# Mixture-of-experts phase: the shared experts moved to the front, their weights loaded and split apart from the routed ones

## The chip, the cores and the metric

One core of a Trainium2 chip runs the whole kernel. The metric is the device time of one execution in microseconds (us); lower is better. "hi" and "lo" below are the two halves into which a float32 tensor is split, so that a product is made by three fp32r matmuls (hi·hi, hi·lo, lo·hi).

## The reference, cut to what matters

The input is `x`, 8 batches of 512 tokens with 256 features. Four layers follow: a mixture of experts, a layer with ternary weights, attention, and a gated feed-forward layer. The change lies in the first.

```
scores = softmax((x @ wt.T + g @ wg.T) / 2)             # 8 routed experts
topk_w, topk_idx = top_k(scores, 2); topk_w /= topk_w.sum(-1)
y_all = (leaky(x @ w_gate[e]) * (x @ w_up[e])) @ w_down[e]
y = sum over the two chosen experts of topk_w * y_all
p = leaky(x @ sw_gate) * (x @ sw_up) @ sw_down          # 2 shared experts of width 128
moe = y + p
```

`leaky(v)` is max(v, 0.01 v). Then `x = x + (quantised moe) @ ternary.T * scale + bias`, and attention and the feed-forward layer follow.

## The kernel before, in words

All ten experts (`NE = 10`: eight routed, `E`, and two shared, `SHARED`) are computed for all tokens, without gathering; a routed expert's activation is multiplied by a per-token weight that is zero where it was not chosen. This is `moe_phase`, a block of its own: the attention phase starts behind a barrier when all engines have ended it. Work is in steps `s = NE*b + k`, batch `b` and expert `k`. Before, k = 0 to 7 are routed and k = 8, 9 are shared. Each engine runs its own list in program order; semaphores join them.

- **TensorE**: `gate_up(b, k)` is 12 matmuls of 512 columns (L33 to L35), into `ps_gate` and `ps_up`, each with two buffers; `down(b, k)` is 12 of 256 columns into `ps_y`, accumulated over all k. `batch` issues `gate_up` two steps ahead: gate_up(k+2), down(k), and then what belongs to other batches (router of b+1 at k = 0, transposes of logits at 1 and of weights at 4, the ternary layer of b-1 at 2, 4, 6). In batch 0 the matmuls `null_projection` (L686) follow down(0,7).
- **ScalarE**: `leak_part` (0.01 v from `ps_gate`, L207), `hidden_hi` (hi half of the hidden activation, L213), and per batch `split_hi` of the next x, `logits_out`, `exps`, `weights_out`, and in batch 0 `projections_hi` (hi half of the attention's query weights, L219).
- **VectorE**: `leaky` (L453, makes `act_g`), `hidden_lo` of the step before (L458), `hidden` (L471, times `ps_up`), and routing (L376 to L418), quantising and the residual (L444).
- **GpSimd**: `weigh` (L300), `act_w = act_g * wide_w` for a routed expert, and `add_bias` (L305), the ternary bias onto `x_nat`, after the eighth `weigh` of a batch. `hidden` of a routed expert waits for its `weigh`; that of a shared one only for `leaky`.
- **SyncE** issues the transfers in order. `load_x`, `load_nat`, then in batch 0 `load_projections` (L834 to L844: query, key-value and output weights and six small tensors of the attention) behind a wait for `raw_free`, then `spread_weights`.

The weights arrive whole: router, gate, up, down (1.25 MB each of the last three). `weight_hi` (L265, ScalarE) and `weight_lo` (L568, VectorE) split each. VectorE does this after the first batch's routing and then unpacks the ternary codes (L583 to L588). `raw_free` comes after that, since the attention's weights take the place of the raw weights in SBUF. TensorE waits for the split gate and up weights before gate_up(0,0), and for the down weights before `batch(0)`.

In batch 0, `null_picks` (VectorE, behind hidden(0,3), L481 and L487) waits for the six small tensors (`att_in`), `null_products` (GpSimd, L314) follows weigh 5 and 7, and `attention_fills` (memsets, L326) follows weigh 2. In batch 6 (`B - 2`), pieces of the attention's first layer norm (`first_norm`, L807 to L827) stand at k = 1, 5, 7 and 9.

Of the kernel before, what the change touches and what calls it, by code (L numbers as in the profile page):

```python
# [11 lines left out]
ALU = mybir.AluOpType  # L12
# [39 lines left out]
def moe_phase(nc, dram, w, ps, sem):  # L52
# [7 lines left out]
    with ExitStack() as ctx:  # L60
        def sb(name, shape, dt=F32):
# [4 lines left out]
        weights = [(router_raw, w.router_hi, w.router_lo, dram.router_t.rearrange("(c p) e -> p c e", p=P)),  # L66
                   (gate_raw, w.gate_hi, w.gate_lo, dram.gate.rearrange("(c p) m -> p c m", p=P)),
                   (up_raw, w.up_hi, w.up_lo, dram.up.rearrange("(c p) m -> p c m", p=P)),
                   (down_raw, w.down_hi, w.down_lo, dram.down.rearrange("(e p) n -> p e n", p=P))]
        ROUTER, GATE, UP, DOWN = range(4)  # L70
# [34 lines left out]
        with nc.Block() as block:  # L105
            @block.sync
            def _(sp):
# [44 lines left out]
                for n, (raw, _, _, src) in enumerate(weights):  # L152
                    sp.dma_start(raw[:], src).then_inc(sem.raw_in[n], 16)
# [16 lines left out]
            def _(act):  # L170
# [63 lines left out]
                def batch(b, par, behind, ahead):  # L234
                    for k in range(NE):
# [3 lines left out]
                        leak_part(s, k % 2)  # L239
# [53 lines left out]
            def _(pool):  # L293
                def weigh(b, k):
                    s = NE * b + k
# [42 lines left out]
                for m in (w.ident, w.ident_bf):  # L338
# [6 lines left out]
                                        pattern=[[-1, E], [1, E]], channel_multiplier=0).then_inc(sem.ident, 1)  # L345
                pool.wait_ge(sem.small_in, 3 * 16)
                for k in range(E):
# [3 lines left out]
                    if k in (5, 7):  # L351
                        null_products(k // 2 - 2)
# [12 lines left out]
            def _(dve):  # L365
# [95 lines left out]
                def hidden(b, k):  # L461
                    s = NE * b + k
                    dve.wait_ge(sem.u_done, s + 1)
                    if k < E:
                        dve.wait_ge(sem.act_w_ready, E * b + k + 1)
# [4 lines left out]
                    src = act_w if k < E else act_g  # L470
# [45 lines left out]
                def batch(b, par, first, behind, ahead):  # L516
                    for k in range(NE):
                        s = NE * b + k
                        leaky(s, k % 2)
                        if not (first and k == 0):  # L520
                            hidden_lo(s - 1, 1 - k % 2)
                        if first and k in (5, 6):
# [12 lines left out]
                        if ahead and k == 0:  # L535
# [5 lines left out]
                        hidden(b, k)  # L541
                        if first and k == 3:
# [22 lines left out]
                def weight_lo(n):  # L565
                    raw, hi, lo, _ = weights[n]
                    dve.wait_ge(sem.hi_ready, n + 1)
                    nc.vector.tensor_tensor(lo[:], raw[:], f32(hi[:]), ALU.subtract).then_inc(sem.lo_ready, 1)  # L568

                split_lo(0, 0)  # L570
                weight_lo(ROUTER)
                softmax_shift(0)
# [4 lines left out]
                weight_lo(GATE)  # L577
                weight_lo(UP)
                weight_lo(DOWN)

                dve.wait_ge(sem.small_in, 3 * 16)
                for c in range(4):
                    nc.vector.tensor_scalar(codes[:, :, c, :], packed[:], 2 * c, 3, ALU.logical_shift_right,  # L583
                                            ALU.bitwise_and)
                dve.drain()
                nc.vector.tensor_scalar(w.tern[:], codes[:].rearrange("p c k n -> p c (k n)"), -1.0, None, ALU.add)
                dve.drain()
                dve.nop(nofuse=True).then_inc(sem.raw_free, 1)  # L588
# [14 lines left out]
            def _(pe):  # L603
# [130 lines left out]
                logits_to_tokens(0)  # L734
# [1729 lines left out]
```

## Time and profile before

| what | value |
|---|---|
| median of 3 runs | 1364.51 us (1364.46 to 1364.55) |
| the profiled execution, its own time | 1364.32 us |
| its span in the profile | 1362.3 us |
| PE busy over the span | 1228.7 us (90%) |
| DVE, ACT, POOL busy | 1035.1, 774.7, 561.9 us |
| moe_phase in the span | 0 to 444 us |

The profile page gives the busy time of each engine. PE is TensorE's matmuls, PEld its weight loads, DVE VectorE, ACT ScalarE, POOL GpSimd, SPq the queue of SyncE. Times in the timeline are microseconds from the span's start; a line has the start, the duration, the engine, the source line, the operation, the tiles (output first), the shape and the count. In brackets stands how long the engine idled before it, and what released it.

### The profile page before, as it was taken

How to read it: one execution, taken by the hardware profiler on the slowest of the kernel's cores; microseconds unless marked ns; L12 is line 12 of the kernel's file. 1: busy time of each engine (PE TensorE's matmuls, PEld its weight loads, DVE VectorE, ACT ScalarE, POOL GpSimd, SP SyncE). 2: the span in 40 equal slices, each digit the busy share in tenths (PEclk: the TensorE clock that was granted, in tenths of full speed). 3: DMA queues.
4: the chain of work that ended last, by engine and by line, in shares of the span. 5: the costliest groups of instructions: out<-in, count | busy, mean ns of one | idle time of the engine just before them, and what ended most of it. 6: DMA issues, size and time to landing. Idle time of an engine off the chain costs nothing. (4 is left out here: it accounts for less than half of the span.)

```text
span 1362.3 us, 26891 instructions
## 1 busy us (share of the span) xinstructions
PE 1228.7 (90%) x8712; PEld 999.2 (73%) x8712; DVE 1035.1 (76%) x2782; ACT 774.7 (57%) x1974; POOL 561.9 (41%) x842
## 2 busy tenths in 40 slices
PE   3999999999887699999999999999999999987976
PEld 2778888888775478788778877887887888764323
DVE  5666666666744777888887897888888887985987
ACT  3333333233232477777677776776777777654666
POOL 1443333323222676435444444454454454530114
PEclk7999999999999699999999999999999999997988
DMA  6332123112200800001001000010010000102206
GB/s 229 118 102 78 52 89 110 71 54 94 89 6 16 290 28 2 1 2 32 1 1 33 1 9 25 2 32 1 1 33 1 1 17 2 65 17 51 62 32 216
DMA packets 49990, 70.38 MB, mean 52 GB/s; under 512 B 4482, under 2 KB 42627, under 8 KB 47812
## 3 DMA queue, kind: packets, MB, share of 16 engines
q1 hardware_dynamic: 49300, 68.55, 15.3%
q8 instruction: 69, 1.13, 0.3%
q14 instruction: 61, 0.50, 0.1%
q10 hardware_dynamic: 560, 0.20, 0.1%
HBM read 56.54 MB, written 12.19 MB: 50 GB/s over the span
## 5 line engine op out<-in xcount | busy, mean ns | idle before, releaser
L1081 POOL TENSOR_SCALAR scores<-scores,att_rinv 128x128 f32<-128x128 f32 (+3 forms) x512 | 266.1, 536 | 175.1 <-DVE att_rinv L1298 175.1
L1142 ACT ACTIVATE scores<-scores,att_top 128x128 f32<-128x128 f32 (+3 forms) x512 | 281.7, 553 | 84.2 <-DVE att_top L1280 83.3
L1280 DVE CUSTOM_DVE_ANT_0 scores<-ps_y,w_bias_b,w_null_s 128x128 f32<-128x128 f32 x448 | 228.4, 547 | 62.5 <-PE ps_y L1475 58.6
L300 POOL TENSOR_TENSOR act_w<-act_g,wide_w 128x512 f32<-128x512 f32 x64 | 105.7, 1652 | 280.0 <-DVE act_g L453 265.4
L1486 PE MATMUL ps_up<-ident,scores 128*128 128x128 f32 x1280 | 191.1, 276 | 9.9 <-DVE keep L1308 5.5
L213 ACT ACTIVATE hid_hi<-hid 128x512 fp32r<-128x512 f32 x80 | 50.6, 632 | 245.9 <-DVE hid L471 245.9
L1486 PEld LDWEIGHTS ps_up<-ident,scores 128*128 128x128 f32 x1280 | 152.7, 141 | 30.5 <-issue 14.4
L1563 PE MATMUL ps_gate<-w_wo,o_t 128*128 128x256 f32 x512 | 133.9, 382 | 0.0
L33 PE MATMUL ps_y<-w_down_hi,hid_hi 128*128 128x256 f32 x320 | 92.6, 289 | 18.1 <-DVE hid_lo L458 18.1
L453 DVE TENSOR_TENSOR act_g<-ps_gate,leak 128x512 f32<-128x512 f32 x80 | 55.3, 691 | 63.2 <-ACT leak L207 60.5
L1142 ACT ACTIVATION_READ_ACCUMULATOR scores<-scores,att_top 128x1 f32 x512 | 96.8, 189 | 0.0
L1150 ACT ACTIVATE keep<-ps_up 128x128 f32<-128x128 f32 (+3 forms) x128 | 55.9, 437 | 62.8 <-PE ps_up L1486 60.2
L1563 PEld LDWEIGHTS ps_gate<-w_wo,o_t 128*128 128x128 f32 x512 | 86.8, 191 | 6.5 <-issue 0.2
L35 PE MATMUL ps_y<-w_down_hi,hid_lo 128*128 128x256 f32 x320 | 90.1, 282 | 0.0
L34 PE MATMUL ps_y<-w_down_lo,hid_hi 128*128 128x256 f32 x320 | 90.0, 281 | 0.0
L1150 ACT ACTIVATE turned_odd<-ps_up 128x128 f32<-128x128 f32 (+3 forms) x128 | 55.9, 437 | 59.4 <-PE ps_up L1486 58.0
L471 DVE TENSOR_TENSOR hid<-ps_up,act_w 128x512 f32<-128x512 f32 x64 | 44.2, 690 | 54.1 <-PE ps_up L35 26.6
L33 PEld LDWEIGHTS ps_y<-w_down_hi,hid_hi 128*128 128x128 f32 x320 | 60.5, 189 | 29.8 <-DVE hid_lo L458 27.5
L1088 POOL TENSOR_SCALAR w_q_hm<-w_q_hl 64x512 fp32r<-64x512 f32 x62 | 37.2, 612 | 103.9 <-ACT w_q_hl L1165 103.9
L1497 PE MATMUL ps_a<-turned_odd,w_val 128*64 128x128 f32 x1280 | 78.6, 279 | 1.3 <-DVE turned_odd L1308 1.3
L1088 POOL TENSOR_SCALAR q_hm<-q_hl 64x512 fp32r<-64x512 f32 x64 | 38.4, 612 | 94.4 <-ACT q_hl L1165 94.4
L1497 PE MATMUL ps_a<-keep,w_val 128*64 128x128 f32 x1280 | 76.9, 275 | 0.0
(335 smaller groups left out, 3226.9 us busy)
## 6 DMA issues: line engine op xcount, KB each, us to landing
wide_w<-token_w_dram SPq DMA_DIRECT2D x16, 1024.0 KB, 4.7
x_raw<-in_x_t_dram SPq DMA_DIRECT2D x8, 512.0 KB, 3.7
x_nat<-in_x_nat_dram SPq DMA_DIRECT2D x8, 512.0 KB, 4.7
x_dram<-x_nat SPq DMA_DIRECT2D x8, 512.0 KB, 2.9
w_x1t<-x_dram SPq DMA_DIRECT2D x8, 512.0 KB, 4.8
x_tile<-x_dram SPq DMA_DIRECT2D x8, 512.0 KB, 4.6
w_bias_b<-in_bias_dram SPq DMA_DIRECT2D x14, 256.0 KB, 4.3
c_dram<-out_raw SPq DMA_DIRECT2D x7, 512.0 KB, 3.2
```

The costliest lines, as they stand in the source:

```text
L33: pe.matmul(out, w_hi, x_hi, start=start, stop=False, skip_group_check=loose)
L34: pe.matmul(out, w_hi, x_lo, start=False, stop=False, skip_group_check=loose)
L35: return pe.matmul(out, w_lo, x_hi, start=False, stop=stop, skip_group_check=loose)
L300: nc.gpsimd.tensor_tensor(act_w[:, k % 2], act_g[:, k % 2], wide_w[:, k], ALU.mult).then_inc(sem.act_w_ready, 1)
L1081: nc.gpsimd.tensor_scalar(s, s, rinv[:, pp, q, hh:hh + 1], 0.0, ALU.mult, ALU.add).then_inc(sem.p_normed, 1)
L1088: nc.gpsimd.tensor_scalar(q_hm[par][0:D, hh], f32(q_hl[par][0:D, hh]), 1.0, 0.0, ALU.mult, ALU.add).then_inc(sem.qm_ready, 1)
L1142: nc.scalar.activation(s, s, ACT.Exp, scale=-1.0, bias=top[:, pp, q, hh:hh + 1], accum_out=lsum[:, pp, q, hh:hh + 1]).then_inc(sem.exp_don ...
L1150: nc.scalar.activation(turned_of(j, 0, 0, cols), psT[:, 0, 0:cols], ACT.Copy).then_inc(sem.pa_ready, 1)
L1280: dve.tensor_tensor_reduce(scores_of(pp, hh, q), psS[:, hh, 0:n], bias_of(w, h)[:, CAUSAL[q]:CAUSAL[q] + n], 1.0, null_s[:, par, q, h:h + ...
L1486: last = pe.transpose(psT[:, hh, k * P:(k + 1) * P], s[:, k * P:(k + 1) * P], w.ident[:])
L1497: last = pe.matmul(psO[hh * D:(hh + 1) * D, cols], val[:, par, k], turned_of(at, hh, k, P), start=(k == 0), stop=(k == q))
L1563: last = pe.matmul(out, o_t[:, p % 2, cols], w.wo[:, p], start=(p == 0 and i == 0), stop=False, skip_group_check=True)
```

## The change

1. The shared experts become k = 0 and 1, the routed ones k = 2 to 9. So `weigh`, and `add_bias` behind the last of them, come two steps later, and `hidden` waits for `weigh` at k ≥ 2.
2. Gate, up and down weights are laid out with the shared experts' columns first, and are loaded and split in two parts each: the shared part (128x512), then the routed part (128x2048). The shared parts are split ahead of the first batch's softmax; TensorE runs gate_up(0,0) before the transposes of the routing weights.
3. The routed gate and up parts' lo halves are made by VectorE after hidden(0,0), followed by `split_lo` of x(1). The routed down part's lo half is made by GpSimd.
4. The ternary codes are unpacked at k = 2 of batch 0, so `raw_free` comes there; it also waits for GpSimd's part. `projections_hi` goes from k = 2, 3 to 3, 4. `null_products` follows weigh 3 and 5, which is the same s as before.

```diff
-        weights = [(router_raw, ...), (gate_raw, ...), (up_raw, ...), (down_raw, ...)]
+        weights = [(router_raw[:], w.router_hi[:], w.router_lo[:], dram.router_t.rearrange("(c p) e -> p c e", p=P))]
+        for first, end in ((0, SHARED), (SHARED, NE)):
+            cols = slice(first * M, end * M)
+            weights += [(gate_raw[:, :, cols], w.gate_hi[:, :, cols], w.gate_lo[:, :, cols], dram_gate[:, :, cols]),
+                        (up_raw[:, :, cols], w.up_hi[:, :, cols], w.up_lo[:, :, cols], dram_up[:, :, cols]),
+                        (down_raw[:, first:end], w.down_hi[:, first:end], w.down_lo[:, first:end],
+                         dram_down[:, first:end])]
+        ROUTER, GATE, UP, DOWN, GATE_ROUTED, UP_ROUTED, DOWN_ROUTED = range(7)
@@ ScalarE, batch
-                        leak_part(s, k % 2)
+                        if behind or k:
+                            leak_part(s, k % 2)
-                        if not behind and k == 2:
+                        if not behind and k == 3:
                             projections_hi(0)
-                        if not behind and k == 3:
+                        if not behind and k == 4:
                             projections_hi(1)
@@ ScalarE, start
+                weight_hi(GATE)
+                weight_hi(UP)
+                weight_hi(DOWN)
                 logits_out(0)
                 exps(0)
-                weight_hi(GATE)
-                weight_hi(UP)
+                weight_hi(GATE_ROUTED)
+                weight_hi(UP_ROUTED)
+                leak_part(0, 0)
+                weight_hi(DOWN_ROUTED)
                 weights_out(0)
-                weight_hi(DOWN)
@@ GpSimd
-                    s = NE * b + k
+                    s = NE * b + SHARED + k
+                pool.wait_ge(sem.hi_ready, DOWN_ROUTED + 1)
+                raw, hi, lo, _ = weights[DOWN_ROUTED]
+                nc.gpsimd.tensor_tensor(lo, raw, f32(hi), ALU.subtract).then_inc(sem.down_lo_ready, 1)
                 for k in range(E):
                     weigh(0, k)
-                    if k in (5, 7):
-                        null_products(k // 2 - 2)
+                    if k in (3, 5):
+                        null_products(k // 2 - 1)
@@ VectorE, hidden
-                    if k < E:
-                        dve.wait_ge(sem.act_w_ready, E * b + k + 1)
+                    if k >= SHARED:
+                        dve.wait_ge(sem.act_w_ready, E * b + k - SHARED + 1)
@@ VectorE, batch
+                        if first and k == 2:
+                            ternary_codes()
-                        if ahead and k == 0:
+                        if ahead and k == 0 and not first:
                             split_lo(b + 1, 1 - par)
                         hidden(b, k)
+                        if first and k == 0:
+                            weight_lo(GATE_ROUTED)
+                            weight_lo(UP_ROUTED)
+                            split_lo(1, 1)
@@ VectorE, start
+                def ternary_codes():
...
+                    dve.wait_ge(sem.down_lo_ready, 1)
+                    dve.nop(nofuse=True).then_inc(sem.raw_free, 1)
                 weight_lo(ROUTER)
+                weight_lo(GATE)
+                weight_lo(UP)
+                weight_lo(DOWN)
                 softmax_shift(0)
                 route_scores(0)
                 route_ranks()
                 route_weights()
-                weight_lo(GATE)
-                weight_lo(UP)
-                weight_lo(DOWN)
@@ TensorE
+                        if not behind and k == SHARED:
+                            pe.wait_ge(sem.down_lo_ready, 1)
                         down(b, k)
@@ TensorE, start
                 logits_to_tokens(0)
+                pe.wait_ge(sem.lo_ready, DOWN + 1)
+                gate_up(0, 0, 0)
                 weights_to_experts(0)
-                pe.wait_ge(sem.lo_ready, UP + 1)
-                gate_up(0, 0, 0)
                 gate_up(0, 1, 0)
-                pe.wait_ge(sem.lo_ready, DOWN + 1)
+                pe.wait_ge(sem.lo_ready, UP_ROUTED + 1)
                 batch(0, 0, False, True)
```

## Rows read from the trace of the kernel before

**Rows 1.** Busy time by stage: PE, PEld, DVE, ACT, POOL, then granted clock, DMA share, GB/s

```profile
0.00:36.00 36.00, 15.01 (x53) 10.05 (x54) 18.61 (x31) 13.33 (x14) 4.57 (x12) 0.81 0.67 236
36.00:90.00 54.00, 48.60 (x260) 37.84 (x258) 34.92 (x55) 15.55 (x28) 23.22 (x16) 0.97 0.31 106
90.00:350.00 260.00, 253.36 (x1478) 213.30 (x1476) 178.69 (x351) 85.25 (x144) 89.51 (x60) 1.00 0.22 76
350.00:444.00 94.00, 75.33 (x426) 61.19 (x426) 52.11 (x102) 26.25 (x44) 23.91 (x15) 0.94 0.11 40
```

**Rows 2.** Timeline of the start, up to down(0,0)

```profile
12.93 0.68 ACT L182 ACTIVATE logit_t<-ps_a,w_cond_half 8x512 f32<-8x512 f32 x1 [4.07 <-PE ps_a L35]
...
16.99 2.32 ACT L265 ACTIVATE w_up_hi<-up_raw 128x2560 fp32r<-128x2560 f32 x1
...
19.59 0.19 DVE L418 TENSOR_TENSOR token_w<-rank,top 128x32 f32<-128x32 f32 x1
...
22.44 2.82 DVE L568 TENSOR_TENSOR w_up_lo<-up_raw,w_up_hi 128x2560 fp32r<-128x2560 f32 x1
...
25.31 0.80 PE L33 MATMUL ps_gate<-x_hi_first,w_gate_hi 128*128 128x512 f32 x1 [4.45 <-DVE w_up_lo L568]
...
35.97 0.28 PE L33 MATMUL ps_y<-w_down_hi,hid_hi 128*128 128x256 f32 x1
```

**Rows 3.** The window of 2 us in down(0,7), columns as in rows 1

```profile
76.00:78.00 2.00, 2.00 (x10) 1.50 (x10) 0.70 (x2) 0.75 (x2) 0.00 (x0) 0.50 0.63 223
```

**Rows 4.** Timeline: VectorE beside GpSimd in batch 0, and down(0,7)

```profile
29.82 1.22 DVE L370 TENSOR_TENSOR x_lo<-x_raw,x_hi 128x1024 fp32r<-128x1024 f32 x1
...
61.98 1.61 POOL L300 TENSOR_TENSOR act_w<-act_g,wide_w 128x512 f32<-128x512 f32 x1 [0.34 <-DVE act_g L453]
...
62.36 2.31 DVE L476 TENSOR_TENSOR w_wq_lo<-keep,w_wq_hi 128x1024 fp32r<-128x1024 f32 x1
...
71.74 2.36 POOL L305 TENSOR_TENSOR x_nat<-x_nat,w_tern_bias 128x1024 f32<-128x1024 f32 x1
...
71.80 2.85 DVE L458 TENSOR_TENSOR hid_lo<-hid,hid_hi 128x512 fp32r<-128x512 f32 x1
...
74.70 0.56 PE L33 MATMUL ps_y<-w_down_hi,hid_hi 128*128 128x256 f32 x1 [2.12 <-DVE hid_lo L458]
```

**Rows 5.** Timeline: the projections' issue, null_picks, projections_hi(1), down(0,3), down(0,4)

```profile
32.00 0.51 SPq L834 DMA_DIRECT2D keep<-in_wq_dram  x1
...
38.81 0.43 SPq L844 DMA_DIRECT2D w_g_out<-in_g_out_dram  x1
...
47.38 0.47 DVE L487 TENSOR_SCALAR w_null_pick<-w_null_pick,w_null_v 64x8 f32<-64x8 f32 x2
...
47.73 1.05 ACT L219 ACTIVATE w_wq_hi<-keep 128x1024 fp32r<-128x1024 f32 x1
...
50.94 0.39 PE L33 MATMUL ps_y<-w_down_hi,hid_hi 128*128 128x256 f32 x1 [0.45 <-DVE hid_lo L458]
...
57.20 0.39 PE L33 MATMUL ps_y<-w_down_hi,hid_hi 128*128 128x256 f32 x1 [0.81 <-DVE hid_lo L458]
```

**Rows 6.** DMA issues of 30 to 50 us: KB, median us from issue to landing

```profile
w_g_out<-in_g_out_dram SPq DMA_DIRECT2D x1, 128.0 KB, 5.5
```

**Rows 7.** Timeline: layer norm pieces on VectorE, batch 6 (k = 7, k = 9), then attention

```profile
361.23 2.26 DVE L821 SCALAR_TENSOR_TENSOR w_work<-w_work 128x4 f32<-128x4 f32 x1
...
370.75 1.55 DVE L827 TENSOR_SCALAR w_x1t<-w_x1t,w_mean_var,w_work 128x256 f32<-128x256 f32 x4
...
704.58 1.12 DVE L827 TENSOR_SCALAR out_raw<-out_raw,w_mean_var,w_work 128x256 f32<-128x256 f32 x2
```

**Rows 8.** Timeline of batch 7: weigh and hidden of k = 7, down(7,9)

```profile
417.68 1.67 POOL L300 TENSOR_TENSOR act_w<-act_g,wide_w 128x512 f32<-128x512 f32 x1 [2.85 <-DVE act_g L453]
...
419.43 0.69 DVE L471 TENSOR_TENSOR hid<-ps_up,act_w 128x512 f32<-128x512 f32 x1 [1.24 <-PE ps_up L35]
...
430.48 0.39 PE L33 MATMUL ps_y<-w_down_hi,hid_hi 128*128 128x256 f32 x1 [0.36 <-DVE hid_lo L458]
```

More of the change, by code:

```diff
@@ L65, in moe_phase @@
         cond_t, router_g, packed, codes = w.cond_t, w.router_g, w.packed, w.codes
[L66 to L70, printed above, removed]
+        dram_gate, dram_up, dram_down = (dram.gate.rearrange("(c p) m -> p c m", p=P),
+                                         dram.up.rearrange("(c p) m -> p c m", p=P),
+                                         dram.down.rearrange("(e p) n -> p e n", p=P))
+        weights = [(router_raw[:], w.router_hi[:], w.router_lo[:], dram.router_t.rearrange("(c p) e -> p c e", p=P))]
[6 more added lines that the diff above has]
+        ROUTER, GATE, UP, DOWN, GATE_ROUTED, UP_ROUTED, DOWN_ROUTED = range(7)
         x_raw = w.x_raw
@@ L152, in _ @@
                 for n, (raw, _, _, src) in enumerate(weights):
-                    sp.dma_start(raw[:], src).then_inc(sem.raw_in[n], 16)
+                    sp.dma_start(raw, src).then_inc(sem.raw_in[n], 16)
                 load_x(1)
@@ L469, in hidden @@
                         dve.wait_ge(sem.hl_ready, s - 1)
-                    src = act_w if k < E else act_g
+                    src = act_w if k >= SHARED else act_g
                     nc.vector.tensor_tensor(hid[:, k % 2], ps.up[:, k % 2], src[:, k % 2], ALU.mult
@@ L567, in weight_lo @@
                     dve.wait_ge(sem.hi_ready, n + 1)
-                    nc.vector.tensor_tensor(lo[:], raw[:], f32(hi[:]), ALU.subtract).then_inc(sem.lo_ready, 1)
+                    nc.vector.tensor_tensor(lo, raw, f32(hi), ALU.subtract).then_inc(sem.lo_ready, 1)
+                def ternary_codes():
+                    dve.wait_ge(sem.small_in, 3 * 16)
+                    for c in range(4):
+                        nc.vector.tensor_scalar(codes[:, :, c, :], packed[:], 2 * c, 3, ALU.logical_shift_right,
+                                                ALU.bitwise_and)
+                    dve.drain()
+                    nc.vector.tensor_scalar(w.tern[:], codes[:].rearrange("p c k n -> p c (k n)"), -1.0, None, ALU.add)
+                    dve.drain()
+                    dve.wait_ge(sem.down_lo_ready, 1)
+                    dve.nop(nofuse=True).then_inc(sem.raw_free, 1)
                 split_lo(0, 0)
                 weight_lo(ROUTER)
+                weight_lo(GATE)
+                weight_lo(UP)
+                weight_lo(DOWN)
                 softmax_shift(0)
@@ L576, in _ @@
                 route_weights()
-                weight_lo(GATE)
-                weight_lo(UP)
-                weight_lo(DOWN)
[L581 to L588, printed above, removed]
                 batch(0, 0, True, False, True)
@@ L2161, in named_semaphores @@
     sem.lo_ready = new("lo_ready")
+    sem.down_lo_ready = new("down_lo_ready")
     sem.cond_logits = new("cond_logits")
@@ L2285, in named_semaphores @@
     sem.out_done = new("out_done")
-    sem.raw_in = [new(f"raw_in{n}") for n in range(4)]
+    sem.raw_in = [new(f"raw_in{n}") for n in range(7)]
     sem.ffn_in = [new(f"ffn_in{n}") for n in range(3)]
@@ L2436 @@
     dram.router_g_t = given("router_g_t", a["L0_cond_wg"].T)
-    dram.gate = given("gate", np.concatenate([e_first(a["L0_cond_w_gate"]), a["L0_cond_sw_gate"]], axis=1))
-    dram.up = given("up", np.concatenate([e_first(a["L0_cond_w_up"]), a["L0_cond_sw_up"]], axis=1))
-    dram.down = given("down", np.concatenate([a["L0_cond_w_down"].reshape(E * M, H), a["L0_cond_sw_down"]], axis=0))
+    dram.gate = given("gate", np.concatenate([a["L0_cond_sw_gate"], e_first(a["L0_cond_w_gate"])], axis=1))
+    dram.up = given("up", np.concatenate([a["L0_cond_sw_up"], e_first(a["L0_cond_w_up"])], axis=1))
+    dram.down = given("down", np.concatenate([a["L0_cond_sw_down"], a["L0_cond_w_down"].reshape(E * M, H)], axis=0))
     dram.packed_t = given("packed_t", a["L0_ffn_packed_weight"].reshape(H // 4, H).T)
```

2 lines of the change are left out of this document (1 added, 1 removed).

## The prediction

> **What bounds the kernel now.** I read the busy time by stage first. `moe_phase` ends at 444 us behind a barrier, and the change touches nothing after it, so the sum is the shift of that end. From 90 to 350 us PE is busy 253.4 of 260 us at full granted clock: there only PE's own work counts, and the change leaves it alone. PE has gaps in three places [rows 1]: the start (15.0 busy of 36), batch 0 (48.6 of 54) and the last two batches (75.3 of 94). The reader is to look for what happens to VectorE and GpSimd there.
>
> In the start PE waits for `w_up_lo`: gate_up(0,0) runs from 25.31, idle 4.45 before, and down(0,0) from 35.97 [rows 2]. The 10.66 us between are three gate_ups, the first at 1.2 GHz (about 5.2), two at 2.4 (2.7 each); so gate_up(0,2) began at 33.25.
>
> One behaviour decides most of what follows. A VectorE instruction with both inputs in SBUF waits for a GpSimd instruction to end, and the other way round. The same 128x1024 subtraction takes 1.22 us alone and 2.31 beside an `act_w` that ends at 63.59; `hidden_lo(7)` takes 2.85 because `x_nat` (2.36 for 128x1024) runs until 74.10 [rows 4]. That held down(0,7) back, idle 2.12, and behind it the granted clock was 0.50, the lower level [rows 3, 4]. From 2.36 per 1024 columns GpSimd needs about 1.2 us for 512 and 4.7 for 2048.
>
> **The start.** The three shared parts cost ScalarE about 0.6 us and VectorE 0.7 each, in gaps that exist (ScalarE idles 4.07 before `logit_t` [rows 2]); three more loads are issued on SP well before its next wait. The routing chain to `token_w` (19.59) stays. gate_up(0,0) now runs beside it. ScalarE: it began the gate's hi half at 14.7, one 2.32 ahead of the up half's; a 2048-column part costs 0.8 of 2.32 = 1.86, so gate, up, leak(0) (0.6) and down end at 14.7 + 5.6 + 0.6 = 20.9. There GpSimd starts the down part's lo half, 4.7 us. VectorE ends leaky(0) and hidden(0) at 21.1 and starts the routed gate and up parts, 0.8 of 2.82 = 2.26 each. Whoever comes first, the three exclude each other: 21.0 + 4.7 + 4.5 = 30.2, not 25.6. gate_up(0,2) starts at 30.2 instead of 33.25, but on a PE that has idled some 5 us. Its price has bounds of 2.7 (2.4 GHz) and 5.2 (1.2 GHz); PE's state after the 4.45 idle is nearest [rows 2], with a rise in part: 4.3. VectorE has hidden_lo(0) ready at 30.2 + 1.2 (x(1)) + 1.4 = 32.8. down(0,0) at 34.5 against 35.97: **-1.5**.
>
> **Batch 0, k = 2 to 4.** VectorE unpacks at k = 2, behind leaky(2), which waits for gate_up(0,2) and leak: 34.0 + 1.3 + unpacking 1.3 gives raw_free at about 36.8. SP passed load_x(2) and load_nat(0) at about 32 and waits there; nobody else is queued behind it that is due. The projections' issue moves from 32.00 to 36.8. Before, the last tensor landed at 38.81 + 5.5 = 44.3, 12.3 us after the first issue, with x(2) and x_nat (1 MB) ahead in the queue [rows 5, 6]; now those are gone, about 3 us at the rates of that stretch. It lands at 46.1; the bounds are 45 and 49.1 (12.3 kept). VectorE reaches null_picks at 43 and waits, which costs most of the lead: it ends at 46.6 instead of 47.85 [rows 5], and down(0,3) comes at 49.4 instead of 50.94: still -1.5. At k = 4 `projections_hi(1)` (1.05, and 0.4 for the key part) now stands on ScalarE ahead of leak(5); before, at k = 3, it lay beside VectorE's routing [rows 5]: **+1.3**. The memsets of `attention_fills` fall beside route_ranks instead of an idle VectorE. No row has a memset beside a two-input instruction, so their price is 0 to 1.1 us (two of the waits that an `act_w` gives); I take 0, nearest to instructions with one SBUF input, which show no wait. The Trainium skill, "SBUF — State Buffer", section "Who interferes with whom", says that a VectorE instruction with two SBUF inputs contends with GpSimd instructions that read SBUF, not with those that only write; by it the sum has 0 here too, while without that distinction it would have 1.1.
>
> **Batch 0, k = 7 to 9.** add_bias comes two steps later, so hidden_lo(7) takes 0.7 instead of 2.85 (-2.2) and down(0,7) keeps the clock (12 matmuls of half the columns of a gate_up's: 1.4 instead of 2.6, -1.2): **-3.4**. At k = 9 hidden now waits for weigh, about 1.2, and add_bias then falls where nothing needs it; batch 1 starts without a weigh: **+0.6** together. Batch 1 begins -3.0 early.
>
> **Batches 1 to 5.** PE-bound. hidden(9) comes 1.2 later, with split_hi behind it on ScalarE, and shows as perhaps 0.2 per batch: **+1.0**.
>
> **Batch 6.** At k = 7 the piece of the layer norm took 2.26 instead of 0.16 behind x_nat [rows 7]; that goes: **-2.1**. At k = 9 the four `tensor_scalar` (1.55 us, with GpSimd idle) now meet weigh(9) and x_nat: a rest of 0.9 and 2.36, **+3.3**. That this form waits too is seen in the attention, where a pair beside GpSimd's scaling took 1.12 against 0.78, half of the four's 1.55 [rows 7].
>
> **The end.** In batch 7, k = 8 and 9 have no gate_up ahead to hide behind. A routed hidden stands 1.24 idle for its act_w (1.67) [rows 8]; a shared one follows at once. s = 78: +1.3; s = 79: +1.3 again. Then x_nat starts as act_w(9) ends; hidden and hidden_hi (1.4) run beside it and hidden_lo waits the remaining 0.9. down(7,9) at about 434 instead of 430.48 [rows 8]: **+3.5**. Nothing covers it.
>
> **Sum.** -1.5 + 1.3 - 3.4 + 0.6 = -3.0; + 1.0 - 2.1 + 3.3 + 3.5 = **+2.7**. On the profiled execution, 1364.32 (span 1362.3 and 2.0 around it), that is 1367.0; it stands 0.2 below the median of the runs, 1364.51. The margin of 0.2% (2.7 us, about what a measurement of this kernel can tell from no change) lies just at it.
>
> **Rivals.**
> A. *The lock isn't seen at the start.* If VectorE runs its two halves without letting GpSimd between, PE starts gate_up(0,2) at 25.6 and raw_free comes 5.5 earlier, so null_picks doesn't wait. It decides from the order of two arrivals, 20.9 and 21.1. For it: they are 0.2 apart. Against: at 62.36 VectorE's subtraction came right behind another and `act_w`, waiting since 61.98, still went first [rows 4]. Price: another 4.6 of lead; 1362.4.
> B. *The late collision doesn't bite:* the four tensor_scalars pass by GpSimd, -3.3; 1363.7. The 1.12 speaks against it. A and B together: 1359.1.
> C. *The null tensors are late, slower.* If they land 12.3 after the first issue (49.1), VectorE stands 6 us, PE idles over 3 at down(0,3), and the clock falls as it did after 2.12 [rows 3, 4]: 3.0 + 1.7, so 1371.7. It decides from a landing after 46. The memsets' 1.1 would come on top.
> D. The change does not do what it says: TensorE's start isn't moved, since the wait for the routed halves remains. That is already most of my case: the lead at down(0,0) is 1.5, not 8.
>
> **Chances.** My case 0.52 (+0.5 to +5: half within, half above 0.2%); A 0.15, B 0.13, both 0.07; C 0.13. Faster by over 0.2%: 0.22, from A and B together, a third of A and of B, and unknown small gains. Within: 0.38. Slower: 0.40. The range 1360.5 to 1371.5 takes in A, B and C's edge.
>
> **What would show it.** In the trace after: GpSimd's 128x2048 subtraction at 20.9, and one VectorE half beside it at 6 to 7 us instead of 2.3; gate_up(0,2) near 30.2; `w_null_pick` behind a wait for the DMA until 46; hidden_lo(7) at 0.7; L827 in batch 6 at 4 to 5 us; the last act_w in batch 7 near 430 and down(7,9) near 434; the block's end near 447. I am wrong if gate_up(0,2) starts by 26, if down(0,3) comes after 52, or if the last steps of batch 7 are no longer than before.

## The result, and the profile after

The changed kernel takes **1374.2 us** (median of 1373.5, 1374.2, 1374.2 and 1378.3) against 1364.53 us of the kernel before on the same chip: ratio 1.0079, 95% interval 1.0066 to 1.0092. The forecast was 1367.0, its range ended at 1371.5. The direction of the likeliest case was right, the size wrong by 7.2 us, and the time lies outside the range. The profiled execution took 1373.53 us, span 1371.6, which is 9.3 us more than the span before. The tables below split those 9.3.

Busy time by stage of the changed kernel (columns as in rows 1, whose four stages it repeats):

```profile
0.00:36.00 36.00, 18.12 (x56) 12.41 (x57) 22.26 (x32) 14.56 (x19) 7.17 (x12) 0.86 0.66 232
36.00:90.00 54.00, 48.22 (x258) 37.83 (x257) 33.69 (x58) 14.64 (x27) 22.38 (x15) 0.97 0.30 99
90.00:350.00 260.00, 253.30 (x1475) 212.12 (x1474) 172.42 (x348) 85.35 (x144) 88.05 (x58) 1.00 0.25 78
350.00:444.00 94.00, 75.01 (x419) 61.12 (x418) 52.54 (x99) 25.53 (x44) 27.80 (x17) 0.95 0.12 40
```

PE is 3.1 us busier in the first 36 us, as the change intends, and by these sums batch 0 and the last two batches look as before. A stage view hides the rest; the place of one matmul in both traces shows it. Start of the first matmul of down(b, k), after minus before, in us:

| down | (0,0) | (0,3) | (0,4) | (0,6) | (0,7) | (0,8) | (1,0) | (1,4) | (6,0) | (6,4) | (6,7) | (6,9) | (7,7) | (7,9) | attention's first |
|---|---|---|---|---|---|---|---|---|---|---|---|---|---|---|---|
| shift | -0.8 | +0.7 | +2.0 | +2.0 | -0.2 | -1.7 | -1.2 | -2.2 | -0.2 | +0.6 | -1.4 | +2.0 | +2.0 | +5.3 | +5.3 |

Behind the attention's first matmul (449.84, before 444.50) the rest of the span is 921.8 us, before 917.8: another **+4.0**, where the forecast had nothing.

Timeline of the changed kernel (start, duration, engine; rows 2, 4 and 5 hold their counterparts):

```profile
20.91 4.56 POOL L359 TENSOR_TENSOR w_down_lo<-down_raw,w_down_hi 128x2048 fp32r<-128x2048 f32 x1 [18.50 <-ACT w_down_hi L272]
21.20 6.43 DVE L588 TENSOR_TENSOR w_gate_lo<-gate_raw,w_gate_hi 128x2048 fp32r<-128x2048 f32 x1
27.55 2.28 DVE L588 TENSOR_TENSOR w_up_lo<-up_raw,w_up_hi 128x2048 fp32r<-128x2048 f32 x1
...
29.88 0.79 PE L33 MATMUL ps_gate<-x_hi_first,w_gate_hi 128*128 128x512 f32 x1 [6.59 <-DVE w_up_lo L588]
...
35.15 1.71 DVE L593 TENSOR_SCALAR codes<-packed 128x128 int32<-128x128 int32 x4
...
42.83 0.43 SPq L868 DMA_DIRECT2D w_g_out<-in_g_out_dram  x1
...
48.12 0.47 DVE L501 TENSOR_SCALAR w_null_pick<-w_null_pick,w_null_v 64x8 f32<-64x8 f32 x2 [3.86 <-DMA w_g_out<-in_g_out_dram]
...
51.65 0.39 PE L33 MATMUL ps_y<-w_down_hi,hid_hi 128*128 128x256 f32 x1 [1.58 <-DVE hid_lo L472]
...
59.16 0.38 PE L33 MATMUL ps_y<-w_down_hi,hid_hi 128*128 128x256 f32 x1 [2.07 <-DVE hid_lo L472]
...
73.76 0.68 DVE L472 TENSOR_TENSOR hid_lo<-hid,hid_hi 128x512 fp32r<-128x512 f32 x1
...
370.64 4.41 DVE L851 TENSOR_SCALAR w_x1t<-w_x1t,w_mean_var,w_work 128x256 f32<-128x256 f32 x4
...
371.65 2.43 POOL L316 TENSOR_TENSOR x_nat<-x_nat,w_tern_bias 128x1024 f32<-128x1024 f32 x1
...
375.71 0.50 PE L33 MATMUL ps_up<-x_hi,w_up_hi 128*128 128x512 f32 x1 [2.09 <-DVE hid L485]
...
431.81 0.51 PE L33 MATMUL ps_y<-w_down_hi,hid_hi 128*128 128x256 f32 x1 [2.72 <-DVE hid_lo L472]
...
434.37 1.39 DVE L472 TENSOR_TENSOR hid_lo<-hid,hid_hi 128x512 fp32r<-128x512 f32 x1 [0.69 <-ACT hid_hi L219]
...
435.81 0.39 PE L33 MATMUL ps_y<-w_down_hi,hid_hi 128*128 128x256 f32 x1 [1.14 <-DVE hid_lo L472]
...
449.84 0.55 PE L1498 MATMUL ps_y<-w_k_hh,w_q_hl 128*128 128x256 f32 x1 [1.93 <-PEq L111]
...
475.55 2.06 POOL L1105 TENSOR_SCALAR scores<-scores,att_rinv 128x256 f32<-128x256 f32 x4
477.58 1.25 POOL L808 TENSOR_SCALAR w_bias_b<-w_bias_b 128x1280 f32<-128x1280 f32 x1
475.58 3.84 DVE L851 TENSOR_SCALAR w_x1t<-w_x1t,w_mean_var,w_work 128x256 f32<-128x256 f32 x2
479.57 0.98 PE L1535 MATMUL ps_a<-ident,w_x1t 128*128 128x128 f32 x4 [3.00 <-DVE w_x1t L851]
```

The first three rows are the lock of the forecast: `w_gate_lo` takes 6.43 us beside GpSimd's 4.56, its twin `w_up_lo` 2.28. The four `codes` took 1.71 us beside an `act_w`, 0.63 in the kernel before. `w_null_pick` waits 3.86 us for a transfer, `hid_lo(7)` is down to 0.68 from 2.85, the four layer-norm instructions of batch 6 take 4.41, and the last two downs wait 2.72 and 1.14 (1.40 and 0.36 before). The last four rows are new: in the attention, two instructions on `w_x1t` take 3.84 us instead of 1.18, and PE stands 3.00 us for them. Some 30 us on, the granted clock falls to the lower level for most of 4 us (0.57; in the kernel before it is 1.00 in this window):

```profile
509.84:513.84 4.00, 4.00 (x20) 0.57 0.02 4
```

### The profile page after: what moved, and what is told of

Read it like the earlier page. It is cut to its first block and busy times, and to the rows that moved or that the text cites. A ratio compares the mean times of both kernels' runs of the same rounds, so it can differ in the third digit from the quotient of the medians.

```text
span 1371.6 us, 26897 instructions
## 1 busy us (share of the span) xinstructions
PE 1232.1 (90%) x8707; PEld 1002.0 (73%) x8712; DVE 1035.8 (76%) x2784; ACT 775.2 (57%) x1977; POOL 567.8 (41%) x843
```

## The experiments

Four theories came out of this. **T1**: GpSimd's subtraction makes `w_gate_lo` late. **T2**: the null tensors, and the projections' hi parts one step later, cost the lead in batch 0. **S**: each part of the change acts where it stands; the shared-first order itself costs at step 9 of batch 6 and at the end. **L**: the 4 us behind the block come from one collision in the attention, which tenths of a us decide (the runs bear out the collision and not the tenths, see runs 2 and 3). "Shift" is down(1,4) against the kernel before; "rest" is the span behind the attention's first matmul.

| run | shift | attention's first | rest | median us | before us | ratio (95%) |
|---|---|---|---|---|---|---|
| before | 0 | 444.5 | 917.8 | | 1364.5 | |
| changed | -2.2 | 449.8 | 921.8 | 1374.2 | 1364.5 | 1.0079 (1.0066 to 1.0092) |
| 1 order alone | -6.4 | 446.6 | 917.7 | 1367.9 | 1364.2 | 1.0033 (1.0019 to 1.0048) |
| 2 batch 0 alone | -0.4 | 444.4 | 922.0 | 1369.9 | 1364.2 | 1.0044 (1.0030 to 1.0059) |
| 3 VectorE's w_down_lo | -3.4 | 449.6 | 919.8 | 1369.9 | 1364.2 | 1.0038 (1.0023 to 1.0052) |
| 4 bias early | -2.5 | 451.3 | 922.5 | 1373.8 | 1364.2 | 1.0064 (1.0047 to 1.0081) |
| 5 before, pair late | +0.3 | 446.0 | 923.5 | 1370.7 | 1364.8 | 1.0045 (1.0028 to 1.0062) |
| 6 pairs together | -2.6 | 451.9 | 920.1 | 1373.3 | 1364.8 | 1.0060 (1.0042 to 1.0078) |
| 7 codes early | -5.2 | 447.4 | 921.9 | 1370.9 | 1364.8 | 1.0050 (1.0033 to 1.0067) |
| 8 first combination | -5.6 | 440.4 | 921.9 | 1363.0 | 1364.8 | 0.9988 (0.9978 to 0.9998) |
| 9 pair early, once | -2.5 | 452.2 | 917.8 | 1371.9 | 1364.2 | 1.0065 (1.0048 to 1.0082) |
| 10 before, batch 0 | -3.5 | 442.2 | 917.4 | 1361.3 | 1364.2 | 0.9978 (0.9968 to 0.9987) |
| 11 second combination | -6.1 | 441.2 | 918.8 | 1359.7 | 1364.2 | 0.9968 (0.9958 to 0.9979) |
| 12 the same, steps 3, 4 | -5.6 | 439.2 | 919.0 | 1359.5 | 1364.2 | 0.9969 (0.9957 to 0.9980) |

Each row's places are of one execution; executions of one kernel spread over some 4 us on the chips of these runs (the kernel before: 1362.3 to 1365.9 in 20), so differences of places are read from the traces and those of times from the medians. The ratios' intervals of runs 4, 6, 7 and 9 overlap that of the changed kernel: their medians alone do not tell them from it. In the block too there is scatter: the lower granted clock cost every run but 2 and 12 some 1.4 to 1.6 us in batch 7, and the changed kernel's profiled execution and the one before 0.3 or less (last section).

**1. The order alone.** The kernel before with

```diff
-                    s = NE * b + k
+                    s = NE * b + SHARED + k
-                    if k in (5, 7):
-                        null_products(k // 2 - 2)
+                    if k in (3, 5):
+                        null_products(k // 2 - 1)
```

and the shared experts' columns first in `dram.gate`, `up` and `down`.

> The kernel before with the shared experts first in every batch and nothing else of the change (weights come whole, the start and the projections' copies stand where they stood, the null products at steps 5 and 7 of the batch, after the third and fifth of its weighed experts). Theory S, each part acts where its work stands: batch 0 is as before up to step 6 (down(0,6) at 68.1 +- 0.3), gains some 4 us at its steps 7 to 9, loses 7.5 us from batch 1 to the block's end (1.3 in batches 1 to 5, 3.0 in batch 6, 3.3 in the last three steps), so that the attention's first matmul starts 3.3 us later than in the kernel before (447.8), and the time is 1367.8 with an attention as before, 1371.8 if the attention grows by 4 us as it did in the changed kernel. Rival P: the loss is the start's, and what is late there pushes the block's stalls about; then this kernel is within 1.5 us of the kernel before at 444.5. Rival A for the attention: what the attention takes depends on when the block ends; the rest behind its first matmul is then anything from 917.8 to 922, not tied to the code, which is the same in all kernels here.

Up to the block's end S held, with a larger gain in batch 0: down(0,6) is already 2.3 us early (not as before), down(0,9) 4.8, and 5.5 to 6.4 in batch 1. From down(1,0) to the attention's first matmul it loses 5.50 + 2.10 = 7.6 us, forecast 7.5; that the two agree is luck, since 1.2 of it are the clock's, between down(7,1) and down(7,4), and batches 1 to 6 lost less than forecast. The stall of step 9 and that of down(7,8) are there although the start is the old one:

```profile
371.10 0.50 PE L33 MATMUL ps_up<-x_hi,w_up_hi 128*128 128x512 f32 x1 [2.02 <-DVE hid L471]
...
428.58 0.58 PE L33 MATMUL ps_y<-w_down_hi,hid_hi 128*128 128x256 f32 x1 [2.72 <-DVE hid_lo L458]
```

So they are the order's, not the start's, and rival P (the start pushes the stalls about) is out.

**2. Shared first in batch 0 alone.** The changed kernel with `s = NE * b + (SHARED if b is 0 else 0) + k` in `weigh`, the like in `hidden`, and `e = k if b is 0 else (k + SHARED) % NE` for the columns in `gate_up` and `down`.

> The changed kernel with the shared experts first in batch 0 alone; batches 1 to 7 take the routed experts first, as before. Theory S: batch 0 as in the changed kernel (down(0,3) 51.7, down(0,6) 70.1, batch 1 some 2.2 us earlier than in the kernel before), then nothing more is lost: the stalls of step 7 come back in batch 6, those of its step 9 and of the last two steps are those of the kernel before, so the attention's first matmul starts 2.2 us earlier than before, at 442.3, and the time is 1362.3 with an attention as before, up to 1366.3 with one of 4 us more. Rival P, the loss in batch 6 and the last steps is the start's doing: the attention's first matmul starts at 447 or later.

From down(1,4) on the shift stays between -0.42 and +0.04 us up to down(7,1): six batches in which only 0.4 us are lost, at down(3,4). S holds for the places, but the lead was 0.4 instead of 2.2 us: the turn to a routed-first batch 1 gave back 0.4 where the changed kernel gained 0.7 from down(0,9) to down(1,0), and at down(1,4) its further gain of 0.9 was missing. The surprise is the rest. The block ends 0.06 us from where it ended before, and yet the attention takes 922.0. This pair of executions is the cleanest sight of L. GpSimd's and VectorE's rows in the kernel before:

```profile
470.03 2.21 POOL L1081 TENSOR_SCALAR scores<-scores,att_rinv 128x256 f32<-128x256 f32 x4
...
470.07 1.18 DVE L827 TENSOR_SCALAR w_x1t<-w_x1t,w_mean_var,w_work 128x256 f32<-128x256 f32 x2
...
471.39 0.63 PE L1511 MATMUL ps_a<-ident,w_x1t 128*128 128x128 f32 x4 [0.36 <-DVE w_x1t L827]
```

and in this one:

```profile
470.14 2.05 POOL L1109 TENSOR_SCALAR scores<-scores,att_rinv 128x256 f32<-128x256 f32 x4
472.17 1.25 POOL L812 TENSOR_SCALAR w_bias_b<-w_bias_b 128x1280 f32<-128x1280 f32 x1
...
470.16 3.84 DVE L855 TENSOR_SCALAR w_x1t<-w_x1t,w_mean_var,w_work 128x256 f32<-128x256 f32 x2
```

Both times VectorE comes a few hundredths after GpSimd's first of four. In the one it is let in behind the first, in the other behind the four and the next instruction, at 473.4. The arrival does not decide this: in the four kernels where VectorE was let in (before, 1, 3, 10) it came 0.03 to 0.04 us after GpSimd's first, in the four where it waited for all (changed, 2, 4, 7) 0.02 to 0.04, and the attention's first matmul stood anywhere from 442 to 450 us in the one group and from 444 to 451 in the other.

**3. VectorE makes the routed `w_down_lo`.**

```diff
-                pool.wait_ge(sem.hi_ready, DOWN_ROUTED + 1)
-                raw, hi, lo, _ = weights[DOWN_ROUTED]
-                nc.gpsimd.tensor_tensor(lo, raw, f32(hi), ALU.subtract).then_inc(sem.down_lo_ready, 1)
...
                             split_lo(1, 1)
+                            weight_lo(DOWN_ROUTED)
```

> The changed kernel with the routed experts' w_down_lo made by VectorE behind x_lo(1), in place of GpSimd's subtraction. Theory T1, GpSimd's subtraction of 4.56 us stretched VectorE's w_gate_lo from about 2.3 to 6.43 us: w_gate_lo takes 2.2 to 2.4 us, gate_up(0,2) starts at 25.6 to 26 in place of 29.88, down(0,0) near 31.5, the projections' transfers are issued some 3.5 us earlier, and down(0,3) starts near 48; the gain goes through to the block's end, 3 to 4 us, time 1370.5 with the same attention. Rival: VectorE's extra 2.3 us in front of leaky(1) and hid_lo(0) takes the gain back (down(0,0) still at 35), or the step 3 wait for the null tensors does not move since their transfers take longer; then the time is within 1 us of the changed kernel's 1374.2.

```profile
21.23 2.28 DVE L586 TENSOR_TENSOR w_gate_lo<-gate_raw,w_gate_hi 128x2048 fp32r<-128x2048 f32 x1
23.43 2.29 DVE L586 TENSOR_TENSOR w_up_lo<-up_raw,w_up_hi 128x2048 fp32r<-128x2048 f32 x1
...
25.77 0.50 PE L33 MATMUL ps_gate<-x_hi_first,w_gate_hi 128*128 128x512 f32 x1 [2.46 <-DVE w_up_lo L586]
...
46.97 0.47 DVE L498 TENSOR_SCALAR w_null_pick<-w_null_pick,w_null_v 64x8 f32<-64x8 f32 x2 [6.00 <-DMA w_g_out<-in_g_out_dram]
...
50.51 0.58 PE L33 MATMUL ps_y<-w_down_hi,hid_hi 128*128 128x256 f32 x1 [5.54 <-DVE hid_lo L469]
```

T1 is shown: with the edit `w_gate_lo` takes 2.28 us, gate_up(0,2) at 25.77, down(0,0) 4.9 us earlier than in the changed kernel. But only 1.1 of the 4.9 are left at down(0,3): the null tensors land 1.1 us earlier and no more (their first transfer is issued 1.9 earlier, at 35.58), since the unpacking that frees the raw weights stood in step 2 all the same. The wait grew from 3.86 to 6.00 us. Start and landing are two limits in a row, which is T2. So the time, 1369.9, met T1's 1370.5 by luck: the block ended only 0.2 us earlier in the profiled execution, and 2.0 of its 2.2 are in the attention, where the pair is let in again:

```profile
474.83 2.22 POOL L1102 TENSOR_SCALAR scores<-scores,att_rinv 128x256 f32<-128x256 f32 x4
...
474.86 1.18 DVE L848 TENSOR_SCALAR w_x1t<-w_x1t,w_mean_var,w_work 128x256 f32<-128x256 f32 x2
```

The edit takes an instruction from GpSimd's list 450 us upstream. Of the eight kernels with the pair in its place, the four in which GpSimd makes `w_down_lo` (changed, 2, 4, 7) have the long wait, and the four in which it does not (before, 1, 3, 10) have the short one. What links the two was not tried: a change of GpSimd's list that leaves its work alone would tell.

**4. The bias earlier in batches 2 to 7** (after the weighing of k = 3 in place of k = 7).

> The changed kernel with GpSimd's addition of the bias to x_nat after the fourth weighed expert of a batch (step 5) in batches 2 to 7, in place of after the eighth (step 9). Theory S: the idle of 2.09 and 0.81 us at step 9 of batch 6 goes (it comes from the layer norm's two-pointer instructions on VectorE beside GpSimd's weigh and x_nat), and that of 2.72 at down(7,8) shrinks by about 1 us; the 0.4 to 0.8 us at step 9 of batches 2 to 5 go or move to step 5. Attention's first matmul 447 to 445.5 in place of 449.84, time 1370 to 1371.5 with the same attention. Rival: the stalls belong to the weighed hidden activations themselves (weigh stands right ahead of the last hidden), and taking x_nat away leaves them: 1373.5 to 1374.5.

S was right on one half alone. Step 9 of batch 6 shrinks (1.3 us lost from down(6,8) to down(6,9) instead of 3.4), and down(7,9) waits 0.37 instead of 1.14; down(7,8) still waits 2.71. But moved to step 5, `x_nat` meets the layer norm's middle piece there, and down(6,5) comes 2.1 us late:

```profile
351.62 2.37 POOL L316 TENSOR_TENSOR x_nat<-x_nat,w_tern_bias 128x1024 f32<-128x1024 f32 x1
...
351.76 2.26 DVE L840 TENSOR_SCALAR w_seed<-w_work 128x4 int32<-128x4 int32 x1
```

That is rows 7's 2.26 of step 7 again, on another instruction. GpSimd's 2.4 us costs about the same at each step where VectorE has such a piece.

**5. The kernel before with its pair asked for later**: three small writes with drains ahead of the second pair in `norm_in`.

> The kernel before, with three writes of zeros to a dead 128x4 tile (each with a drain, together an estimated 0.3 to 0.5 us, from the 0.06 to 0.17 us of VectorE's small instructions) ahead of the second pair of the layer norm's subtract-and-multiply instructions on w_x1t in the attention loop. Everything up to the attention's first matmul is unchanged (444.50 +- 0.2). Theory L: whether that pair (470.07 in the kernel before, 1.18 us) is let in behind the first of GpSimd's four back-to-back scores instructions (470.03) or only behind all of them and the w_bias_b instruction after them is a matter of tenths of a us; asked for some 0.4 us later it waits for the chain, takes 3 us or more, the clock falls near 505 as in the changed kernel, and the rest behind the attention's first matmul grows from 917.8 to 920.5 to 922: 1367 to 1368.5. Rival A: the 4 us have another source (the block's code or the end of the block), and 0.4 us on VectorE at this place are hidden: 1364 to 1365.

```profile
471.56 2.19 POOL L1081 TENSOR_SCALAR scores<-scores,att_rinv 128x256 f32<-128x256 f32 x4
473.72 1.25 POOL L784 TENSOR_SCALAR w_bias_b<-w_bias_b 128x1280 f32<-128x1280 f32 x1
...
471.98 3.14 DVE L827 TENSOR_SCALAR w_x1t<-w_x1t,w_mean_var,w_work 128x256 f32<-128x256 f32 x2
```

Asked for 0.42 us behind the first of the four, the pair's first instruction gets in behind the second of them, and its second waits for the two left and `w_bias_b`, until 474.97. The time rises by 5.9 us, more than L said. In the profiled execution 1.5 stand in the block, at down(7,3), where the edit is not (the clock). Of the rest's 5.7 us, 1.5 are there by 480 us, another 3.5 come bit by bit in the attention loop, where the same edit stands six times more, and 1.6 near 1220, of which 0.9 come back. That the clock would fall near 505 was wrong here (1.00 in 500:520). The rival, that 0.4 us are hidden here, is out; that tenths of a us made the difference between the two kernels is not shown by it.

**6 and 9. The pair beside the first pair, where GpSimd is idle**; in 6 in all batches of the attention, `NORM_IN = (2, 2, 3, 3, 4, 4, 5, 5)`, in 9 in its first alone.

> The changed kernel with the attention's second pair on w_x1t one step of its schedule earlier, right behind the first pair (NORM_IN ends 5, 5 in place of 5, 6): GpSimd is idle there. Theory L: the pair of 3.84 us is gone, the clock does not fall near 510 (granted 1.00 in 500:520, 0.91 in the changed kernel), the rest behind the attention's first matmul falls from 921.8 to 917.5 to 919, time 1370 to 1371.5 in place of 1374.2; the attention's first matmul stays at 449.8. Rival A: the 4 us stay, 1373.5 to 1374.5.

> The changed kernel with the second pair on w_x1t one step earlier in the attention's first batch alone (in the run that had it in all seven, 1.9 us came back between 510 and 1100 us). Theory L, sized by that run: at the attention's first matmul the block is as in the changed kernel (449 to 452, by where the clock falls in batch 7), the pair waits for nothing, the granted clock of 500:520 is 1.00, and the rest behind that matmul is 917 to 919 (917.8 of the kernel before, less 1.0, more 0.3, and 1.5 more if the clock falls near 1225): time 1369 to 1371.5. Rival A: the rest stays above 921 and the time at 1373.5 to 1374.5.

In 6 the collision and the fall of the clock near 510 were gone and the rest was 4.0 us ahead of the changed kernel's at 510 us, but 1.9 came back in the loop, where the changed kernel lost 0.3, so the time was only about 1 us less: above what L said. In 9, with the edit in one batch, the rest was 917.8 as in the kernel before. Run 9's four instructions with no wait in them, and its window of 500 to 520 us (the changed kernel's: 18.06 busy, 0.91):

```profile
473.88 1.55 DVE L851 TENSOR_SCALAR w_x1t<-w_x1t,w_mean_var,w_work 128x256 f32<-128x256 f32 x4
```

```profile
500.00:520.00 20.00, 17.87 (x133) 1.00 0.00 1
```

This is what shows L's collision: moving two instructions of 0.4 us takes 3.9 us off the rest, and all of it stands already at 510 us. (From 1200 us to the end the changed kernel lost 0.7 and run 9 0.9.) The total, 1371.9, fell by less, since the block ended 2.3 us later in that execution: its clock fell beside step 4 of batch 7 (below).

**7. The codes early**: `ternary_codes()` behind `weight_lo(DOWN)` of the start, `raw_free` behind `split_lo(1, 1)`.

> The changed kernel with the ternary codes made behind w_down_lo of the shared experts (at 11.9, where VectorE then waits 2.4 us for the logits) in place of step 2, and raw_free given behind x_lo(1), at 31.1 in place of 37.4. Theory T2, the loss of 1.1 us at down(0,3) and of part of the 1.25 us at down(0,4) is the null tensors' landing: they land near 42 in place of 48.1, down(0,3) has no idle over 0.5 us and starts at 50.5 or earlier in place of 51.65, down(0,4) at 57.6 or earlier in place of 59.16, and batch 1 and all behind it come 1.1 to 2.4 us earlier: time 1371.8 to 1373.1 with the same attention. Rival: what holds step 3 is VectorE's own list (null_picks and hid_lo), then down(0,3) stays within 0.4 us of 51.65; or the codes delay the routing (two groups of instructions ahead of the logits' maximum) and gate_up(0,2) starts 0.5 us later.

```profile
45.14 0.47 DVE L501 TENSOR_SCALAR w_null_pick<-w_null_pick,w_null_v 64x8 f32<-64x8 f32 x2 [2.12 <-DMA w_g_out<-in_g_out_dram]
...
56.19 0.39 PE L33 MATMUL ps_y<-w_down_hi,hid_hi 128*128 128x256 f32 x1 [2.06 <-DVE hid_lo L472]
```

T2's first half is shown: down(0,3) at 48.7 without idle, 3.0 us earlier than in the changed kernel, all of which reaches batch 1. The landing came at 45.1, not 42: the weights are free at 31.2, but the first transfer is issued at 32.20, right behind those of x(2) and x_nat as in the kernel before [rows 5], so 5.3 us of earlier issue gave 3.0 of earlier landing. The wait at down(0,4) is unchanged (2.06 against 2.07), so it is not the landing's.

**8, 11 and 12. The findings together.** 8 is 2 + 3 + 7 with the pairs of 6. In 11 the pair moves in the first batch alone and `projections_hi` is back at k = 2 and 3; 12 is 11 with it at k = 3 and 4.

> A version that puts the findings together: the changed kernel with the shared experts first in batch 0 alone, the routed w_down_lo made by VectorE, the codes early and raw_free behind w_down_lo (near 29.2), and the attention's pair one step earlier. Theories T1, T2, S and L together: down(0,0) at 30.3, down(0,3) at 45.5 to 46.5, down(0,6) 5 us earlier than in the kernel before, batch 1 on 6 to 7 us earlier and flat from there on, the attention's first matmul at 438 and the rest 917.5 to 919: time 1357 to 1359, 5.5 to 7.5 us under the kernel before. Rival: the start's gain is taken by the projections as in the run with VectorE's w_down_lo (-5.5 at down(0,2), +0.8 at down(0,4)); then 1362 to 1364.

> The version of the run before that beat the kernel before (shared first in batch 0 alone, VectorE's w_down_lo, codes early, raw_free behind w_down_lo), with two edits: the pair one step earlier in the attention's first batch alone, and the projections' hi parts back at steps 2 and 3 of batch 0. Theory H (the hi parts one step later cost the 2.07 us of idle at down(0,4), which is 0.8 with them at steps 2 and 3): down(0,3) at 45.5 to 46.5, down(0,4) at 50.5 to 51.5 in place of 53.5, down(0,6) 6 us earlier than in the kernel before, the attention's first matmul at 436.5 to 439, the rest 917 to 921: time 1356 to 1360. Rival: w_wq_raw has not landed by step 2 (issued near 30, transfers of 8 us), ScalarE waits for it with the leak parts and hid_hi queued behind, and down(0,3) starts 1 to 2 us later: no gain over the next run.

> The same with the projections' hi parts at steps 3 and 4, as the change has them. Against the run before it this is the price of that step: down(0,4) at 53.5 with 2.07 us of idle, batch 1 at -5.6 us, attention's first matmul at 438.9 to 440.5, the rest 917 to 921, time 1358 to 1362; 1 to 2.4 us more than with steps 2 and 3 under theory H, no more than 0.3 us under the rival.

8 has the rival's price in the block and the worse rest, 1363.0. Its pairs wait for nothing, and by 490 us it is 1.1 ahead of the kernel before; then the clock falls all the same (0.72 in 496:502, 1.00 in 494:500 before), which costs 1.0, and 2.4 are lost in the loop and 1.4 near 1220. Down(0,3) and down(0,4) in 11:

```profile
46.82 0.39 PE L33 MATMUL ps_y<-w_down_hi,hid_hi 128*128 128x256 f32 x1 [1.19 <-DVE hid_lo L469]
53.08 0.38 PE L33 MATMUL ps_y<-w_down_hi,hid_hi 128*128 128x256 f32 x1 [0.81 <-DVE hid_lo L469]
```

and in 12:

```profile
45.87 0.39 PE L33 MATMUL ps_y<-w_down_hi,hid_hi 128*128 128x256 f32 x1 [0.70 <-DVE hid_lo L469]
53.38 0.38 PE L33 MATMUL ps_y<-w_down_hi,hid_hi 128*128 128x256 f32 x1 [2.06 <-DVE hid_lo L469]
```

The hi parts at step 4 cost exactly 1.25 us at down(0,4); at steps 2 and 3 ScalarE waits 2.27 us for the transfer, and down(0,3) is 0.95 later. The net is 0.3 us there and nothing in the medians, so the rival has it. 11 and 12 are the fastest versions, 4.5 us under the kernel before.

**10. The kernel before, shared first in batch 0 alone**, nothing else of the change but the null products.

> The kernel before (its weights whole, its start, its projections' steps) with the shared experts first in batch 0 alone, the null products at steps 5 and 7. Theory S: batch 0 goes as in the run with the order alone (down(0,6) 2.3 us, down(0,9) 4.8 us earlier than before), the turn to batch 1 gives back 0.4 us, and all from there to the block's end stays 4.3 to 4.6 us earlier: the attention's first matmul at 440 to 441.5, the rest 917.7 to 922 by the pair and the clock: time 1360 to 1364.5. Rival: the 6 us gained by step 4 of batch 1 in the run with the order alone were the shared-first order of batch 1; then less than 2 us are left at down(1,4).

3.5 us early at down(1,4) and at down(7,1), 2.9 us gained in the median; less lead than the 4.3 of theory S, since down(0,6) was 1.6 instead of 2.3 us early. The attention's first matmul is 2.3 us early: 1.2 went to the clock between down(7,1) and down(7,4). It beats the kernel before by the order of one batch.

## Why the prediction was wrong, by its own steps

**The step that failed is "the change touches nothing after it, so the sum is the shift of that end."** The code behind the block is the same, and yet 4.0 of the 9.3 us are there: 1.9 by 480 us from the pair on `w_x1t`, 1.0 near 510 and 1.4 near 1220 where the granted clock is lower (0.66 in 1220:1230, before 0.83 at the same place, 1211:1221), and 0.3 in the loop between, less 0.7 gained behind 1220. Runs 2, 3, 5, 6 and 9 pin the first down to the wait of the pair; why the changed kernel has that wait and the kernel before not stays open. The second was there in the runs with the long wait (2, 4, 7) and absent (1.00 in 500:520) in 1, 3, 6 and 9 to 12, but absent in run 5, which has the wait, and there in run 8, which has not: the wait does not settle it. What starts the falls near 510 and 1220 was not tried.

**The start: mechanism right.** Lock seen, GpSimd at 20.9, gate_up(0,2) at 29.88 (forecast 30.2). Its price came out higher: in the profiled execution all twelve matmuls ran at the lower clock (0.50 in 29.5:35.5), 5.3 us in place of 4.3, so -0.8 and not -1.5. In runs 2, 4, 6 and 9, whose start is the same, it was 4.6 to 4.8 and down(0,0) came at -1.25 to -1.53: there the forecast held. Rival A was out.

**Steps 2 to 4: mis-sized; 2.2 us of the block's error stand at down(0,3).** They are the landing's and not the start's: with the better start of runs 2, 4, 6 and 9 it came at +0.3 to +0.5. Raw_free came at 37.4 (36.8 forecast), since the codes stood beside an `act_w`: 1.71 us. The null tensors landed at 48.1, not 46.1: the forecast took 3 us off the 12.3 for the transfers no longer ahead, and measured are about 10.7 behind raw_free. down(0,3) came at +0.7, not -1.5. This was rival C in part: its mark ("from a landing after 46") was met, but PE idled 1.58 there, not over 3, and the clock did not fall at down(0,3). The +1.3 for `projections_hi(1)` was right: 1.25 from down(0,3) to down(0,4), and again between runs 11 and 12. The 0 for the memsets was right too: VectorE's instruction with two SBUF inputs takes 1.51 beside an `act_w`, and 0.42 and 0.43 (at 53.60) beside a memset:

```profile
51.52 1.51 DVE L412 TENSOR_TENSOR ge<-ge,gt 128x256 f32<-128x256 f32 x1
...
52.86 0.95 POOL L337 MEMSET w_q_hm<- 64x1024 f32 x1
...
53.10 0.42 DVE L414 TENSOR_TENSOR ge<-ge,w_earlier 128x256 f32<-128x256 f32 x1
```

**Steps 7 to 9: right.** -3.4 forecast; from down(0,6) to down(0,8) -3.7. The +0.6 of step 9 and the turn to batch 1 was 0.5. Batch 1 began 1.2 early, not 3.0.

**Batches 1 to 5:** +1.0 forecast, +1.0 measured from (1,0) to (6,0), but by luck: it is made of +0.6 to +1.1 from each step 8 to the next batch's step 0, where the forecast had 0.2, and of -0.5 to -0.9 at each step 4, which it did not see. **Batch 6:** -2.1 measured at step 7, -2.1 forecast; +3.4 at step 9, +3.3 forecast. The form of rows 7 does wait. Not seen was +0.7 at down(6,4), where up(6,6) waits 1.07 instead of 0.49. **The end:** +3.5 forecast, +3.3 measured between down(7,7) and down(7,9).

**The sum of the block**: 2.7 forecast, 5.3 measured; 1.8 of the 2.6 missing are batch 0, 0.7 down(6,4). The mechanisms it named were all there; the range broke because it was drawn around these alone, and 2.6 of block and 4.0 of attention went the same way. With the rule cited for memsets (the Trainium skill, "SBUF — State Buffer", section "Who interferes with whom") the trace agrees, by the rows above (1.51 beside an instruction that reads SBUF, 0.42 beside one that only writes it). The same section says that whoever issues first holds the shared ports for its whole instruction and the other blocks; the 6.43 us beside 4.56 agree.

## What to carry to other kernels

Ask of each early gain which limit stands next in line and move that too: the start's 5 us were worth 1 until the transfers' release moved with them (run 3; in run 8, with both moved, 4.9 of 5.3 are left at down(0,3)). An order of work that helps where a pipeline fills may cost where it drains, and can be had in the filling batch alone (runs 1, 2 and 10). Where two engines that exclude each other run dense lists, a change far upstream can pick another outcome downstream (1.18 or 3.84 us for the same pair here), so a forecast of 0.2% needs a term for it on both sides, and an instruction that is exposed to it should stand where the other engine is idle (run 9).

## What the runs showed of the hardware that was not expected

- **Between back-to-back instructions of one engine the other gets in or not, and not by when it comes.** With GpSimd's chain begun 0.02 to 0.04 us earlier, VectorE's pair waited for five instructions in the changed kernel and runs 2, 4 and 7 (3.84 us in the first two), and for one in the kernel before and runs 1, 3 and 10 (1.18 us). Begun 0.42 us earlier (run 5), it let one instruction of the pair in and held the other. What decides was not found.
- **Small integer instructions wait too.** Four `codes` of 128x128 int32 take 0.62 us alone (run 7) and 1.71 beside an `act_w`.
- **Whether a fall of the clock costs depends on what runs then.** In batch 7 of the kernel before it fell at 388 us (0.57 in 388.5:392.5), behind a stretch in which PE was busy 1.22 of 3.4 us, beside gate_up matmuls issued in step 1, and cost 0.3 us at down(7,2), which waits for VectorE anyway. In run 1 it fell behind down(7,3), 13 us later, and cost 1.4 us at down(7,4). All runs but 2 and 12 lost 1.4 to 1.6 us at down(7,3) or down(7,4), and runs 4 and 11 another 1 us at down(7,2). What moves the fall was not tried. The window of run 1 in which it fell (1.00 in the kernel before):

```profile
400.00:406.00 6.00, 5.92 (x27) 0.72 0.00 1
```
